# A four-layer graph network on one core: logits in column tiles, edge work on ScalarE and in the first steps, reordered turns with unread products

## The reference, cut to what matters

```
L0: A_hat = normalised(adj + I); h = relu(batchnorm((A_hat x) W1.T + b1)); out = batchnorm(h W2.T + b2)
L1: _, U = eigh(normalised Laplacian(adj)); out = U (relu(U.T x W1 + b1) W2 + b2)
L2: q = x W_lin.T, v = x W_val.T                       # 4 heads, 256 edges src -> dst
    e = a . leaky_relu(q[src] + q[dst], 0.2) + log(adj[src, dst] + 1e-8)
    attn = softmax of e over the edges of one src;  out = (sum over edges of attn * v[dst]) W_out.T
L3: h = relu(adj (x Wg0 + bg0)); h = relu(adj (h Wg1 + bg1)); four LSTMs over windows of 1 to 4 nodes
```

## Time and profile before

| | us |
|---|---|
| median of 3 runs | 1037.67 |
| lowest, highest | 1037.54, 1038.46 |
| the profiled execution's own time | 1037.68 |
| its span, first to last instruction | 1035.9 |
| TensorE busy | 928.0 |
| VectorE busy | 615.2 |
| ScalarE busy | 603.3 |
| GpSimd busy | 159.2 |

### The profile page before, as it was taken

One profiled execution on the slowest core, in us unless ns is written; L12 is line 12 of the kernel. 1 busy time (PEld: TensorE's weight loads), 2 busy tenths in 40 slices (PEclk: granted clock), 3 DMA queues, 4 the chain that ended last, 5 costly groups with the idle time before them and its releaser, 6 DMA issues.

```text
span 1035.9 us, 13392 instructions
## 1 busy us (share of the span) xinstructions
PE 928.0 (90%) x3987; PEld 606.9 (59%) x3987; DVE 615.2 (59%) x2155; ACT 603.3 (58%) x1520; POOL 159.2 (15%) x458
## 2 busy tenths in 40 slices
PE   3799867878888986999999999999999999999994
PEld 2555554455556664666888777885444466654442
DVE  5577766745668784477445797434544444544676
ACT  0456646736537773277644355535966688875556
POOL 0233333313333332000000000000000000000055
PEclk9799977867779896799999999999999999999998
DMA  9100000000000000000000000000000000000014
GB/s 257 49 1 1 0 1 1 1 1 1 1 1 2 1 1 1 1 1 1 1 1 1 1 2 1 1 1 0 1 1 0 1 0 1 1 0 1 0 41 122
DMA packets 14328, 12.99 MB, mean 13 GB/s; under 512 B 896, under 2 KB 11056, under 8 KB 14256
## 3 DMA queue, kind: packets, MB, share of 16 engines
q1 hardware_dynamic: 14018, 11.98, 4.1%
q10 hardware_dynamic: 238, 0.16, 0.1%
HBM read 7.89 MB, written 4.19 MB: 12 GB/s over the span
## 4 chain that ended last, share of the span: by engine, by line
PE 73%; DVE 16%; ACT 6%; issue 3%; DMA 1%; POOL 1%; ACTq 0%; DVEq 0%; POOLq 0%
PE bank L938 17%; PE bank L962 9%; PE bank L857 3%; PE bank L799 3%; PE bank L789 3%; PE bank L813 3%; PE bank L847 3%; PE bank L620 2%; PE bank L619 2%; PE bank L506 2%; PE bank L753 2%; PE bank L764 2%; PE bank L925 1%; PE bank L865 1%; PE bank L917 1%
## 5 line engine op out<-in xcount | busy, mean ns | idle before, releaser
L1409 ACT ACTIVATE hid_t<-bank,gate_b 128x512 f32<-128x512 f32 (+1 forms) x252 | 148.9, 630 | 48.9 <-PE bank L962 48.2
L1518 POOL TENSOR_SCALAR x<-x,perm 128x128 f32<-128x128 f32 x32 | 29.3, 928 | 592.7 <-DVE perm L2169 592.7
L962 PE MATMUL bank<-ms,w_t 128*128 128x512 f32 (+1 forms) x288 | 110.8, 528 | 0.1
L938 PE MATMUL bank<-hid_t,w_t 128*128 128x336 f32 (+1 forms) x296 | 106.6, 506 | 1.2 <-DVE x L2144 1.2
L938 PE MATMUL bank<-feat_t,w_t 128*128 128x512 f32 x208 | 93.1, 603 | 0.0
L938 PEld LDWEIGHTS bank<-hid_t,w_t 128*128 128x128 f32 x296 | 55.8, 190 | 46.2 <-issue 25.8
L962 PEld LDWEIGHTS bank<-ms,w_t 128*128 128x128 f32 x288 | 54.1, 190 | 48.1 <-issue 33.8
L938 PEld LDWEIGHTS bank<-feat_t,w_t 128*128 128x128 f32 x208 | 39.1, 189 | 51.0 <-issue 46.7
L1197 ACT ACTIVATE con<-bank,con 128x1 f32<-128x1 f32 x62 | 16.2, 261 | 89.3 <-PE bank L620 89.2
L1416 ACT ACTIVATE hid_t<-hid_t 128x512 f32<-128x512 f32 (+1 forms) x72 | 41.8, 581 | 34.9 <-DVE hid_t L2128 25.6
L1043 ACT ACTIVATE x<-x,perm 128x128 f32<-128x128 f32 x128 | 52.3, 482 | 2.6 <-DVE perm L1550 2.6
(11 more groups left out here) (420 smaller groups left out, 2121.7 us busy)
## 6 DMA issues: line engine op xcount, KB each, us to landing
out<-x SPq DMA_DIRECT2D x16, 256.0 KB, 3.0
con<-in_constants SPq DMA_DIRECT2D x1, 449.0 KB, 3.1
feat_t<-in_L_gnn_W SPq DMA_DIRECT2D x2, 128.0 KB, 3.6
e_int<-in_L_gnn_src ACTq DMA_DIRECT2D x1, 128.0 KB
l_w<-in_L_gnn_W SPq DMA_DIRECT2D x2, 64.0 KB
wg<-in_L_gnn_Wg SPq DMA_DIRECT2D x2, 64.0 KB
adj_n<-in_adj SPq DMA_DIRECT2D x1, 64.0 KB, 3.3
x<-in_x SPq DMA_DIRECT2D x4, 0.5 KB, 10.3
```

Source lines behind the costliest of these rows:

```text
L938: return mm(bank[4 * u + BANK_OF[g]][:, 0:w], w_t[:, WB_IH + 4 * (it.p - 1) + g, :], lstm_x(n), start=True, stop=(it.k == 0))
L962: mm(bank[4 * u + BANK_OF[g]][:, 0:w], w_t[:, WB_HH + 4 * (it.p - 1) + g, :], lstm_h_of(it.chain)[:, 0:w], start=False, stop=True).then_in ...
L1409: f(dst[:, 0:w], bank[4 * u + BANK_OF[g]][:, 0:w], ACT.Tanh if g == G_G else ACT.Sigmoid, bias=gate_b[:, 4 * (it.p - 1) + g:4 * (it.p - 1) ...
```

## The change

- L2: `l2_logits` gives each batch of a tile its own 32 rows of the accumulator and a strip of 32 columns; `soft_columns` puts the columns back in order.
- Edges: the one-hot and rank matrices are made on ScalarE (`edge_hots`, from |a - b| and relu); their products move from the preamble into turn 0 (`first_products`, `edges_rows`, `edges_adjacent`, `edges_starts`). What VectorE did at the end of the preamble moves to the start of `layer1` (`edge_rest`). `eig_start` is gone. Buffers that were shared get their own (`kept`, `pair`, `pv_ident`, `square`).
- L0's slots all move one step later; the aggregation waits at first for a quarter of `x` only.
- Turns: in the slot of h2 the work of `beside` is issued ahead of `pe_turn`, not behind it. `dve_next(h1)` goes ahead of `dve_tangents`, and `act_vector` ahead of `act_row_norm`.
- Unread products: `kept_busy` goes. `filled` issues 384 columns ahead of `pe_rows(h2)` and 384 ahead of `pe_turn` in every turn (turn 0 has the second alone), 384 and 128 in each slot without L0 products (23, 40 to 44, 61 to 63), and some at the end of the eigenvectors.

```
-A_AGG, A_COPY, A_HID0, A_HID1, A_SAVE0, A_SAVE1, A_STATS = 0, 1, 1, 2, 2, 2, 4
+A_AGG, A_COPY, A_HID0, A_HID1, A_SAVE0, A_SAVE1, A_STATS = 1, 2, 2, 3, 3, 3, 5
...
+            def first_products(h0):
+                edges_sources()
+                pe_rows(h0)
+                pe_w(0)
+                edges_targets()
+                pe_rank(h0)
+                pe_off(0)
+                pe_diagonals(0)
+                edges_ends()
...
                 pe_rows(h1)
-                kept_busy(h1)
+                if i == 0:
+                    edges_rows()
                 beside(h1)
                 pe_rank(h1)
                 behind_rank(h1)
+                if i == 0:
+                    edges_adjacent()
+                    edges_starts()
+                else:
+                    filled(384, True)
                 pe_rows(h2)
-                kept_busy(h2)
+                beside(h2)
+                filled(384, False)
                 pe_turn(i)
-                beside(h2)
                 pe_rank(h2)
...
-                for k in range(2):
-                    pe.wait_ge(s["l2_act"], 2 * t + k + 1)
-                    rhs = ht[k][:, :, :].rearrange("p a b -> p (a b)")
-                    for b in range(2):
-                        r = HEADS * (TB * (t % PAIRS) + 2 * k + b)
-                        d = mm(bank[6 + half][:, 0:E], head_strip[:, P - HEADS - r:2 * P - HEADS - r], rhs[:, b * E:(b + 1) * E],
-                               start=(r == 0), stop=(r == P - HEADS))
+                pe.wait_ge(s["l2_act"], 2 * t + 2)
+                at_ = HEADS * (t % PAIRS)
+                for b in range(TB):
+                    rhs = ht[b // 2][:, :, :].rearrange("p a b -> p (a b)")
+                    d = mm(bank[6 + half][DH * b:DH * (b + 1), 0:E], head_strip[:, P - HEADS - at_:P - HEADS - at_ + DH],
+                           rhs[:, b % 2 * E:(b % 2 + 1) * E], start=(t % PAIRS == 0), stop=(t % PAIRS == PAIRS - 1))
...
+            def edge_columns(k, to):
+                away = pen_b if k else pen_f
+                for c in range(EC):
+                    link.mark(f(away[:, c * P:(c + 1) * P], iota[:, 0:P], ACT.Abs, scale=-1.0, bias=s_col[:, EC * k + c:EC * k + c + 1]))
+                link.settle()
+                for c in range(EC):
+                    f(to[:, c, :], away[:, c * P:(c + 1) * P], ACT.Relu, scale=-1.0, bias=ones[:, 0:1])
...
+                if i == 0:
+                    edges_sorted()
                 dve_dif(i)
                 beside(h0)
                 dve_sum(i)
                 dve_reflected(h1)
+                dve_next(h1)
                 dve_tangents(i)
-                dve_next(h1)
```

More of the change, by code:

```diff
@@ L114, in steps_of, with without_products @@
     return [first + n for n in range(4)] + [first + 4 if turn in POLISHED else None]
+def without_products(slot):
+    taken = [A_HID0, A_HID1, A_AGG, B_OUT, C_TURN]
+    return slot not in TURN_AT and not any(0 <= slot - first < TILES for first in taken)
 BATCHES = {1: 4, 2: 8, 3: 8, 4: 16}
@@ L279, in graph_layers @@
         jdif, jdsq, josq, jsign = w_sb[:, :], diag_mat[:, :], scaled[:, :], u_nat[:, :]
[L280 to L281 removed]
+        jabs, jhyp, jos, jt = [t[:, k * P:(k + 1) * P] for t in (con_f, con_b) for k in range(2)]
+        jb, jx, jy_sb = src_b[:, 0, :], src_b[:, 1, :], square[:, :]
         jv1_sb, jb0, jp1, jy2_sb, jf_sb, jm = jdif, jdsq, josq, jabs, jhyp, jt
@@ L461, in edges @@
[L461 to L467, removed]
+                    mm(bank[3][:, 0:E], src_1h[:, c, :], perm[:, c, :], start=(c == 0), stop=(c == EC - 1))
@@ L546, in behind_rank, with filled, kept_busy @@
                     l0_hidden(slot - A_HID0, 0)
[L548 to L552, removed]
+            def filled(cols, rows_read):
+                into = bank[5] if rows_read else bank[6]
+                mm(into[:, P:P + cols], ident, con[:, 0:cols], start=True, stop=True)
+            def kept_busy():
+                filled(384, False)
             def pe_w(i):
@@ new lines, in edge_places @@
+            def edge_places():
+                away = con_f, con_b
+                act.wait_ge(s["edge_cols"], 4)
+                for c in range(EC):
+                    link.mark(f(perm[:, c, :], sum_st[:, :], ACT.Sign, bias=rank[:, 0, c:c + 1], accum_out=rank[:, 1, c:c + 1]))
+                link.settle()
+                act.wait_ge(s["edge_cols"], 5)
+                for c in range(EC):
+                    link.mark(f(away[c][:, :], iota2, ACT.Abs, bias=rank[:, 1, c:c + 1]))
+                link.settle()
+                for c in range(EC):
+                    t = f(perm[:, c, :], away[c][:, :], ACT.Relu, scale=-0.5, bias=ones[:, 0:1])
+                t.then_inc(s["edge_hot"], 1)
@@ new lines, in edge_hots, with edges_spread @@
+            def edge_hots():
+                act.wait_ge(s["edge_cols"], 3)
+                edge_columns(0, src_1h)
+                edge_places()
+                edge_columns(1, dst_1h)
+                for c in range(EC):
+                    t = f(src_b[:, c, :], ones[:, :], ACT.Copy, scale=s_col[:, c:c + 1])
+                t.then_inc(s["edge_hot"], 1)
+            def edges_spread():
+                act.wait_ge(s["edge_sorted"], 2)
+                f(dst_st[:, :], bank[7][:, 0:E], ACT.Copy)
+                f(src_s[:, :, :], bank[7][:, E:2 * E], ACT.Copy).then_inc(s["edge_act"], 1)
@@ L2201, in _ @@
             dve.memset(ones[:, :], 1.0).then_inc(s["ones_set"], 1)
+            dve.memset(rows[:, :, :], 0.0)
+            dve.memset(kept[:, :, :], 0.0)
+            dve.memset(eps_col, EPS)
+            link(dve.memset(pair[:, :], 0.0))
             graph_matrices()
-            columns()
-            edges()
+            eigen_setup()
             eigenvectors()
```

235 lines of the change are left out of this document (123 added, 112 removed).

## The result

| | before | after |
|---|---|---|
| median, us | 1038.07 | 982.33 |
| lowest, highest | 1037.54, 1038.98 | 981.57, 984.10 |
| the profiled execution's own time | 1037.68 | 983.05 |
| its span | 1035.9 | 981.2 |
| TensorE busy | 928.0 | 900.8 |

The changed kernel takes 0.9465 of the time, with an interval of 0.9448 to 0.9481. That is 55.7 us less, against 34.5 forecast: the range of 984 to 1024 missed it by 1.7.

A forecast was written before the change was run, and what follows sets the result against it. TensorE was taken as the bound, in a stage of latencies with a varying clock before about 430 us, then all TensorE. From 1037.68: -14.5 - 2 - 12 + 4 - 1 - 5 - 0.5 - 3.5 = -34.5, so 1003.2; range 984 to 1024.

The forecast's parts named there:

- The preamble: Start up to the first `pe_rank`: ScalarE's `av` copy at 15.0 us, first `pe_rank` at 18.5 instead of 33.06; -14.5 us.
- Turn 0: First eigenvector turn: TensorE's work continuous from 12.5 us on, half of the 4.1 us over turn 2 given back; -2.
- The step h2: Turns: products moved ahead of `pe_turn` fill TensorE's wait, so `pe_rank` starts earlier; 12 x 1.0, -12 us.
- It decides in both orders: 0: The two swaps on VectorE and ScalarE in the turns: `src_b` decides in either order, so 0 us.
- The unread products and the clock: Turns and slots: added unread products +4, vanished ones -1; less time at TensorE's 1.2 GHz -5 us.
- an eighth of the cost: Clock term: of some 40 us that 1.2 GHz costs in clock slices 2 to 15, an eighth goes: 5 us.
- L2 (-3.5): Logit blocks of L2: 1.48 us for 1.73, sixteen times, less 0.5 for finer copies in `soft_columns`.
- rival 1: L2: the four column tiles run wholly side by side, block 0.83 us, L2 gives 12, total 994.5; chance 20.
- The staircase: L2 logit block: one tile's second record runs beside the next tile's first, five steps instead of eight, 1.08 us.
- Rival 2: Turns: clock stays low in h2, reordering gives 0, unread products cost 10; 1027, or 1015 with half affected; chance 20.
- Rival 3: Slower: unread products lie on the path at 1.2 GHz, +31, tile changes +6.4; 1059 or 1048; chance 5.
- Rival 4: Preamble: ScalarE's matrices so slow that it gains little, mattering only with `av` at 27 us; no separate chance given.

The follow-up runs named there:

- the experiment: Changed kernel without the unread products in the turns and in the slots without L0 products (those at the end stay): 999.92 us, ratio 0.9634.
- the second attempt at more: Changed kernel with the batch norm's square roots behind the step's own work, plus more unread products in three late places: 982.39 us, ratio 0.9458.
- both attempts at more: Changed kernel with the batch norm's square roots behind the step's own work, 981.52 us; the same with more unread products, 982.39 us.

## Why the prediction was wrong

Three steps of the prediction failed. The logit block of L2 was counted as five products one behind the other where four and four ran side by side (-3.5 forecast, -13.7 in the table). The clock's term was far too small and stood apart from the order's, which turned out to work through the clock. And the swaps were counted as nothing. Term by term:

**The preamble (-14.5) was right**: 15.4. Ten of ScalarE's matrices at 0.31 and the rest at 0.38 were near enough (0.34 and 0.49). That it would be kept was right only in company: alone it leaves 11.5 by the medians and 13.6 by the profiled executions.

**Turn 0 (-2)** gave 3.5 in this execution, nearly all of the 4.1 that I halved, and as much in two others. In the eight other profiled executions with the early start it gave 0.6 to 1.9 (last section), so -2 lay between, and that it did is luck: the forecast had no term for what sets the two apart.

**The step h2 (-12)** is 15.6 shorter, but not for the reason I gave. The term was the order's: 1.0 a turn, twelve times, by a wait that ends. Read at one clock on both sides, the order gives 0.47 in four turns and takes nearly as much in the first four, 0.3 in all. These fifteen steps spent 39.5 us less at 1.2 GHz than before (27.2 for 66.7, from the length of each step and its clock), and that shortened them. Either edit alone does much of it, with the swaps in both cases: the new order without unread products has 33.4 us at 1.2 GHz in these steps (89.8 us long in sum), the old order with them 22.4 (89.5 long), against 101.6 long before and 86.0 now. So the order's gain is of the clock's kind, which the term didn't contain. I had taken the gap of one step at a mixed clock (turn 12, L521 at 1.49) for the gap of all.

**"It decides in both orders: 0"** failed. I asked whether the swap moves `src_b` and forgot its other end: `dve_next(h1)` makes the column on which step h1 itself waits. The runs give 7, of which 3.8 is seen directly, some 0.47 in each of eight turns.

**The unread products and the clock (+4, -1, -5)** failed in size: -2 forecast. The 17.6 of the experiment is against none of them and so is not this term. By the table the turns gave 18.9; less the 0.3 of the order and the 3.8 of the swaps that are seen at equal clock, some 15 are left for it, an estimate by difference; no run makes the exchange of the unread products alone. The 124 us at 1.2 GHz and their 40 us of cost were a fair start. The choice of "an eighth of the cost" had no row behind it, and the "28 x 0.65" beside it doesn't follow from the counts given (23 before, 38 and nine short ones after); it is in no sum. From turn 1 to the last `pe_rank` the time at the low level fell by two fifths (2 x 0.16 x 344.9 = 110 to 65 us), and two fifths of 40 are 16. A further 2.5 is in L1, where I forecast nothing: before, the low clock of the eigenvectors' end lasted into it (0.96 over its 62.6 us), a row that the prediction doesn't have.

**L2 (-3.5)** failed in its mechanism. "Five steps instead of eight" is wrong: the records are four first ones together and four second ones together, a block of 0.57 and 0.2 to 0.26 on its neighbour, 0.9 less per block. Sixteen of them less 0.5 for the copies are 13.9; the trace shows 12.7 in the stretch and 1.0 for the last block behind it. That is rival 1, which I gave 20 and priced at 12. The rule that products start and end in program order, which the Trainium skill states in "TensorE: Matmul & The Clock Gate", The mechanism, agrees with the trace: the eight start one behind the other, the first four within 20 ns. The staircase was my own inference from it, that a tile's second record would hold up the next tile's first. The figure of the Trainium skill's same page for three column tiles, 2.38 times (Measured speedup vs the span model), led to an estimate of 0.58 for the block, and the trace has 0.57.

**The rivals.** Rival 1 is what L2 did; its 994.5 (its own terms give 994.7) left the clock's term as small as mine, which is why it fell short too. Rival 2 holds in part in six turns (5 and 11 to 15), whose steps h2 still meet the low clock for 3.4 to 6.9 us. Rival 3 never occurred: without the unread products the kernel is slower. Rival 4 didn't either.

## What to carry to other kernels

- Products that write different 32-column tiles and don't depend on one another run side by side, also as two-record float32 products: 0.57 us for four, against 1.84 in one tile and 1.73 at full width. The shape change costs 0.2 once per block, so blocks are worth forming.
- In a stage of latencies, a product that nobody reads can be worth more than its time. Here it was where a step had no other filling (nine places: 14 us), and it was worth nothing where the step was already full (15 places: 0). Further ones (the second attempt at more) bought 10 us of the high clock and no time. Price the clock's share from the profile first: time at the low level times what a turn loses by it, and ask which gaps end.
- When two operations on one engine change places, look up what waits for each of the two, not only the join that both feed.

## What the hardware showed unexpectedly

- At the start TensorE runs at half speed for a while, and the profile shows a granted clock of 1.00 there. The same edge product L492, in the changed kernel and in the one with the root moved, where it stands unedited:

```profile
20.77 1.13 PE L492 MATMUL bank<-perm,src_b 128*128 128x256 f32 x4
```

```profile
23.36 2.08 PE L492 MATMUL bank<-perm,src_b 128*128 128x256 f32 x4
```

  In the first, the records of one row of products of 128 columns start 0.21 us apart up to 16.07 and 0.11 apart from there (L474); in the second, products are short only from 25.4 on. The stretch from 17.6 to 23.0 has 1.00 in both. This 1.00 is not a reading. The clock entries of the kept traces begin at 16.1 us in the one and at 25.4 in the other, both times with 2.4 GHz, and what lies ahead of the first entry is counted as 1.00. The length of the products tells the level: the first `pe_rows` takes 0.64 us at 14.0 in the changed kernel, and took 0.63 at 29.56 before, where 0.50 is on record. Turn 0 is 22.7 or 25.4 us long in these two. Each of the fourteen profiled executions begins so. With the early start the first entry comes at 15.8 to 17.4 us in six and at 24.4 to 25.5 in five (tiles' products in one tile, `pe_turn` ahead, both attempts at more, and without the products ahead of `pe_rows`), and which it is does not follow from the edits. With the old start it comes at 22.6 to 24.2, ahead of turn 0, and costs the turn nothing. So up to 2.7 us of a difference between two single profiles may be this, and an early start can lose part of its gain to it.
- The granted clock reacts to small shifts. The executions of one kernel lie up to 11 us apart (987.5 to 998.8), where those of the kernel before lie 1.3 to 4.4 apart in each of four groups. What decides where a low stretch begins was not found out.
- Four two-record products in one 32-column tile took 0.11 us longer than four of full width (1.84 and 1.73), over the same moving data. The change of shape ahead of them may be the reason; no run tells the two apart.
